# Attention with its scores in two pairs of PSUM banks, everything else in one bank, and two transposes moved from TensorE to DMA as 16-bit parts

## The chip, the core and the metric

One core of a Trainium2 chip runs the whole program. Its engines work side by side and wait for each other by semaphores: PE multiplies matrices (PEld is its weight load), DVE (vector), ACT (scalar) and POOL (GpSimd) do elementwise work, and SP only issues DMA transfers, strictly in its own order. PE writes its results to PSUM, 8 banks of 128 partitions x 512 floats; DVE and ACT can read PSUM, POOL and the DMA can't. The metric is the device time of one launch in microseconds (us).

## The reference

```python
x = x + attn(layernorm(x))        # x: 16 sequences x 512 tokens x 256, 16 heads of 16, rotary, causal softmax
x = x + ffn(layernorm(x))         # one shared SwiGLU expert and 8 routed ones, top 2, hidden 512
def attn(x):
    q, k, v = split(x @ W_attn + b_attn)
    att = softmax(where(causal, (rope(q) @ rope(k).T) / 4, -inf))
    return (att @ v) @ W_proj + b_proj
```

Inputs and outputs are float32. Only the attention half and its hand-over to the second half are touched by the change.

## The kernel before

The attention runs over 16 sequences, called batches here and `b` in the code. A batch has 4 groups (`g`) of 4 heads, and a group has 5 steps (`s`), so a batch has 20 steps, written (g, s). Every engine's program is a loop over these steps, and at each step a table says which piece of side work it does there: `QK = ((0, 4), ...)` means that the first of the four query and key projections is issued at step 4 of group 0. The tables fix each engine's order by hand; semaphores do the rest.

At every step PE issues two things first. `scores` computes queries by keys for one unit (128 x 1024) into a pair of banks, `pair_s`; the unit has causal masks added by four small matmuls. DVE takes the row maxima from it (`row_max`), and since there is one pair only, `scores` of the next unit waits for that (`max_done`). `shifted` computes keys by queries again, with the maxima as an extra row, into `pair_t`, for a group issued 8 steps earlier (`LAG = 8`); ACT takes the exponential of it (`exponentials`, to `prob`), and only then may the next `shifted` start (`exp_done`). POOL zeroes what the causal mask hides (`select`), and `mix` on PE multiplies with the values, in four pieces (`MIX`) that wait for the selects.

The maxima go back as a row: `maxima` transposes them on PE into bank 6 (`ps_m`), ACT copies them to float16 (`shift_rows`), and SP writes them with two small DMAs into the operand of `shifted` (`load_shift`).

The side work of a batch: the input of the batch after next is loaded, DVE and POOL take its mean and deviation (POOL's power operation, `input_rstd`), ACT normalises it (`normalise`). For the next batch PE transposes it (`transpose_xn`, 8 matmuls of 128 columns), ACT and DVE split it into a high and a low part of type float32r (`xn_high`, `xn_low`), and PE forms queries, keys and values as three products of the parts (`products`, L1574: 24 matmuls of 512 columns, 24 of 256). POOL splits queries and keys to 16 bits (`qk_high`, `qk_low`), and SP takes them through DRAM into place (`store_qk`, `load_qk`). For the previous batch PE transposes the outputs (`transpose_o`), DVE divides (`divide`), PE transposes back (`transpose_y`), ACT copies (`y_t`), PE multiplies in float32 with `wp` (`project_out`), DVE adds the residual (`residual`), and statistics, normalisation and a store follow. These uses have three banks of their own (`ps_q`, `ps_m`, `ps_y`).

After the last batch the pipeline drains, while SP turns stored rows by DMA for the routing, and then the feed-forward half begins.

Of the kernel before, what the change touches and what calls it, by code (L numbers as in the profile page):

```python
# [43 lines left out]
def build(nc, x, w_attn, b_attn, w_proj, b_proj, ln_scale, ln_bias, gate_w, Wg, Wu, Wd, sWg, sWu, sWd, rope, out):  # L44
# [41 lines left out]
    with ExitStack() as ctx:  # L86
# [68 lines left out]
        xh = sb_a("xh", [P, 2, T], F32R)  # L155
        xl = sb_a("xl", [P, 2, T], F32R)
# [12 lines left out]
        y_t = sb_a("y_t", [P, 2, 2, P], F32)  # L169
# [3 lines left out]
        mvb = sb_a("mvb", [P, 2, 2], F32)  # L173
# [4 lines left out]
               for k in range(2)]  # L178
# [84 lines left out]
        x_loaded = [S["x_in0"], S["x_in1"]]  # L263
        x1_stored = [S["x1_out0"], S["x1_out1"]]
# [3 lines left out]
        XN_BANK, QK_BANK, V_BANK = (ps_q, ps_y), (ps_s[0], ps_s[1], ps_o, ps_q), ps_t  # L268
# [1691 lines left out]
```

## Time and profile before

| | us |
|---|---|
| median of 3 runs (1655.62 to 1658.88) | 1657.58 |
| the profiled execution | 1656.44 |
| its span, first to last instruction | 1654.7 |
| PE busy in the span | 1513.6 |
| DVE busy | 1054.2 |
| ACT busy | 828.8 |
| POOL busy | 898.4 |

The attention takes up the first 785 us or so, the rest is the feed-forward half. Busy shares are averages over both, so the attention has to be read from its own stretch of the trace. PE's matmuls are pipelined: the time that one costs the others is the distance from its start to the start of the next, not its own duration. The other engines' durations may be added up nearly as they stand.

### The profile page before, as it was taken

How to read it: one execution, taken by the hardware profiler on the slowest of the kernel's cores; microseconds unless marked ns; L12 is line 12 of the kernel's file. 1: busy time of each engine (PE TensorE's matmuls, PEld its weight loads, DVE VectorE, ACT ScalarE, POOL GpSimd, SP SyncE). 2: the span in 40 equal slices, each digit the busy share in tenths (PEclk: the TensorE clock that was granted, in tenths of full speed). 3: DMA queues.
4: the chain of work that ended last, by engine and by line, in shares of the span. 5: the costliest groups of instructions: out<-in, count | busy, mean ns of one | idle time of the engine just before them, and what ended most of it. 6: DMA issues, size and time to landing. Idle time of an engine off the chain costs nothing.

```text
span 1654.7 us, 41571 instructions
## 1 busy us (share of the span) xinstructions
PE 1513.6 (91%) x14714; PEld 1103.3 (67%) x14716; DVE 1054.2 (64%) x1852; ACT 828.8 (50%) x1252; POOL 898.4 (54%) x1121
## 2 busy tenths in 40 slices
PE   3689999999999999987698989999999999999995
PEld 2345555555555555543586778888888898888884
DVE  7567888887888888877478777753333333333332
ACT  1266767666666666656132225544444444444442
POOL 2144555554555555544123667736766666666663
PEclk9699999999999999999699999999999999999998
DMA  2323333333233333243866854446766666666563
GB/s 83 96 91 90 116 100 113 103 109 111 90 110 111 109 108 112 91 126 94 185 176 178 194 122 98 107 107 94 109 103 98 100 100 103 99 101 100 100 102 37
DMA packets 283156, 181.03 MB, mean 109 GB/s; under 512 B 160625, under 2 KB 273649, under 8 KB 282962
## 3 DMA queue, kind: packets, MB, share of 16 engines
q1 hardware_dynamic: 244370, 130.25, 30.9%
q0 software_dynamic: 30016, 35.55, 14.6%
q10 hardware_dynamic: 8576, 12.58, 2.4%
q8 instruction: 129, 2.11, 0.6%
q14 instruction: 65, 0.53, 0.1%
HBM read 83.91 MB, written 60.17 MB: 87 GB/s over the span
## 4 chain that ended last, share of the span: by engine, by line
PE 67%; DVE 10%; DMA 8%; SPq 5%; issue 3%; ACT 3%; POOL 3%; DVEq 0%; POOLq 0%; ACTq 0%
PE bank L1574 20%; PE pair_s L1848 13%; PE bank L1709 7%; PE bank L1848 6%; PE pair_t L1848 6%; PE pair_s L1636 4%; SPq L441 3%; PE bank L1744 3%; PE pair_t L1683 3%; DMA qk_d<-qkl 2%; ACT prob L882 2%; DVE early L1501 1%; POOL prob L684 1%; PE pair_s L1656 1%; ACT early L991 1%
## 5 line engine op out<-in xcount | busy, mean ns | idle before, releaser
L882 ACT ACTIVATE prob<-pair_t 128x1024 f32<-128x1024 f32 x320 | 327.4, 1023 | 233.3 <-PE pair_t L1683 228.4
L684 POOL TENSOR_SCALAR_AFFINE_SELECT prob<-prob 128x256 f32<-128x256 f32 (+1 forms) x448 | 198.4, 456 | 334.0 <-ACT prob L882 329.3
L807 POOL DMA_INDIRECT out_x<-ysb,tok_rows x135 | 217.6, 1612 | 158.6 <-ACT ysb L1018 105.2
L991 ACT CAST early<-early 128x512 f16<-128x512 f32 (+1 forms) x206 | 124.3, 603 | 333.6 <-DVE early L1501 333.6
L1507 DVE TENSOR_TENSOR early<-early 128x512 f16<-128x512 f32 (+1 forms) x206 | 139.1, 675 | 137.9 <-ACT early L991 137.3
L1501 DVE SCALAR_TENSOR_TENSOR early<-pair_s,h_s,sg 128x512 f32<-128x512 f32 (+1 forms) x103 | 75.3, 731 | 225.4 <-PE pair_s L1848 223.2
L766 POOL DMA_INDIRECT tok_d<-tok_w,dest_i x128 | 137.1, 1071 | 103.9 <-DVE dest_i L1426 52.8
L1574 PE MATMUL bank<-wbuf,early 128*128 x1620 | 188.7, 273 | 4.6 <-DVE early L1507 2.8
L1848 PE MATMUL pair_s<-xt,wbuf 128*128 128x256 f16 x1704 | 188.7, 267 | 0.0
L1709 PE MATMUL bank<-prob,v_op 128*32 128x512 f32 (+3 forms) x2048 | 179.1, 445 | 5.1 <-POOL prob L684 5.0
L1157 DVE TENSOR_REDUCE mx<-pair_s 128x2 f32<-128x1024 f32 x128 | 156.8, 1225 | 41.1 <-PE pair_s L1656 40.3
L1574 PEld LDWEIGHTS bank<-wbuf,early 128*128 128x128 f16 x1620 | 157.7, 98 | 24.4 <-issue 5.8
L1848 PEld LDWEIGHTS pair_s<-xt,wbuf 128*128 x1704 | 160.3, 98 | 17.5
L785 POOL DMA_INDIRECT xrow<-xhl_d,tok_rows x135 | 137.1, 1015 | 53.1 <-issue 36.6
L1636 PE MATMUL pair_s<-k_op,q_op 48*128 48x512 f16 (+3 forms) x1024 | 128.5, 310 | 34.1 <-DVE mx L1157 12.1
L1636 PEld LDWEIGHTS pair_s<-k_op,q_op 48*128 48x128 f16 x1024 | 34.8, 94 | 153.7 <-DVE mx L1157 70.2
L1683 PE MATMUL pair_t<-q_op,k_op 49*128 49x512 f16 (+3 forms) x1024 | 124.3, 300 | 11.7 <-DMA q_op<-m_row 9.6
L1160 DVE TENSOR_REDUCE mx<-pair_s 128x2 f32<-128x768 f32 x128 | 122.0, 953 | 19.0 <-PE pair_s L1656 17.6
L983 ACT ACTIVATE sg<-pair_s,silu_s 128x512 f32<-128x512 f32 (+1 forms) x103 | 69.1, 671 | 82.9 <-PE pair_s L1848 71.1
L1848 PE MATMUL pair_s<-xrow,wsh 128*128 128x256 f16 x720 | 87.2, 277 | 15.9 <-DVE early L1501 15.8
L1848 PE MATMUL bank<-xt,wbuf 128*128 128x256 f16 (+1 forms) x852 | 100.7, 268 | 0.0
L1848 PE MATMUL pair_t<-xt,wbuf 128*128 128x256 f16 (+1 forms) x852 | 100.2, 267 | 0.0
(273 smaller groups left out, 2742.8 us busy)
## 6 DMA issues: line engine op xcount, KB each, us to landing
q_op<-qk_d SPq DMA_DIRECT2D x192, 64.0 KB, 2.6
k_op<-qk_d SPq DMA_DIRECT2D x192, 64.0 KB, 2.7
x_in<-in_L_attn_x SPq DMA_DIRECT2D x16, 512.0 KB, 3.9
qk_d<-qkh SPq DMA_DIRECT2D x32, 256.0 KB, 2.2
qk_d<-qkl SPq DMA_DIRECT2D x32, 256.0 KB, 2.6
xres<-in_L_attn_x SPq DMA_DIRECT2D x16, 512.0 KB, 4.6
x_d<-x SPq DMA_DIRECT2D x32, 256.0 KB, 2.2
xhl_d<-xhl SPq DMA_DIRECT2D x32, 256.0 KB, 2.5
```

Source lines behind the costliest of these rows:

```text
L684: last = nc.gpsimd.affine_select(out=v, in_=v, compare_op=ALU.is_ge, fill=0.0, base=0, pattern=[[0, v.shape[1]], [1, P]], channel_multipli ...
L766: pool.indirect_dma_start(out=tok_d, out_offset=bass.IndirectOffsetOnAxis(ap=dest_i[:, t, k:k + 1], axis=0), in_=tok_w[:, t, k, :], in_off ...
L807: pool.indirect_dma_start(out=out, out_offset=bass.IndirectOffsetOnAxis(ap=tok_rows[:, block, 0:1], axis=0), in_=ysb[:, here], in_offset=N ...
L882: nc.scalar.activation(prob[:, half, u].rearrange("p a n -> p (a n)"), pair_t[:].rearrange("p a n -> p (a n)"), ACT.Exp, scale=exp_by).the ...
L991: nc.scalar.copy(hth2[:, par, 2 * hh:2 * hh + 2, 0:w], hb2[:, hh, 0:2 * w].rearrange("p (c n) -> p c n", c=2)).then_inc(S["hh_done"], 1)
L1157: last = nc.vector.tensor_reduce(dst[:, :, u, 3], pair_s[:], AX_X, ALU.max)
L1507: nc.vector.tensor_tensor(htl2[:, par, 2 * hh:2 * hh + 2, 0:w], hb2[:, hh, 0:2 * w].rearrange("p (c n) -> p c n", c=2), hth2[:, par, 2 * h ...
L1574: last = nc.tensor.matmul(out, a, m, start=(i == 0), stop=(i == n - 1))
L1636: nc.tensor.matmul(ps_s[a][:, lo:lo + P * (q + 1)], q_op[64 * a:64 * a + KR, par, pair, P * q:P * (q + 1)], k_op[64 * a:64 * a + KR, par, ...
L1683: last = nc.tensor.matmul(ps_t[a][:, lo:lo + n], k_op[rows, par, pair, P * k:P * (k + 1)], q_op[rows, par, pair, P * k:], start=start, sto ...
L1709: last = nc.tensor.matmul(ps_o[32 * h:32 * h + 32, P * k:], v_op[:, vpar, k, GH * gg + h, :], pr[:, unit, h % 2, lo:lo + n], start=(piece ...
L1848: last = nc.tensor.matmul(out[:, w * k:w * k + w], stationary, rows[:, x, 0:w], start=(i == 0), stop=(i == 3 * CC - 1))
```

## The change

1. Banks. The scores alternate between `pair_s` and a second pair, `pair_u`, so `scores` waits for the row maxima of the unit before the last. In exchange `maxima`, `project_qk`, `project_v`, `transpose_o` and `project_out` all use the one bank `ps_a`; each waits until the user before it has been read out.
2. Normalised rows. `transpose_xn`, `xn_high` and `xn_low` go. POOL splits each of the four tiles of `xn` into float16 high and low parts (`xn_split`: a cast and a subtraction), and one DMA transpose on SP (`xn_columns`) turns all of it. The weights' parts are float16 too; the values' weights are scaled as well, and `values` multiplies back.
3. Divided rows. `transpose_y` and the copy to `y_t` go. POOL splits each of four tiles (`y_split`), two DMA transposes a batch turn them (`y_columns`), and `project_out` becomes three float16 products with the split `wp` (24 matmuls of 256 columns a batch). Before the first batch, `output_scales` on DVE finds the scale of `wp`, after another `partition_all_reduce` on POOL.
4. The variances go straight to `mv_all`; the copy to `var_all` goes.
5. All tables are new. `LAG` is 9, `maxima` is at step 1 instead of 0, `mix` at steps 1, 3, 3, 4 instead of 0, 2, 2, 3, the statistics of the next input at (0, 3) and (0, 4) instead of (1, 0) and (1, 2), `input_shift` at (1, 2) instead of (2, 1).

```diff
-        LAG, MAXIMA, M_ROWS, M_SP, O_OUT = 8, 0, 1, 2, 3
-        MIX = (0, 2, 2, 3)
-        QK, QK_ROWS = ((0, 4), (1, 4), (2, 4), (3, 1)), ((1, 0), (2, 0), (3, 0), (3, 4))
+        LAG, MAXIMA, M_ROWS, M_SP, O_OUT = 9, 1, 1, 2, 4
+        MIX = (1, 3, 3, 4)
+        XN_SPLIT, XN_COLUMNS = ((2, 2), (3, 0), (3, 2), (3, 4)), (0, 0)
+        QK, QK_ROWS = ((0, 4), (1, 2), (1, 4), (3, 4)), ((0, 4), (1, 2), (1, 4), (3, 4))
...
+            def xn_split(n, t):
...
+                high = xn_hl[:, t, 0:C]
+                nc.gpsimd.tensor_copy(high, xn[:, t]).then_inc(S["xnh_done"], 1)
+                pool.wait_ge(S["xnh_done"], NT * n + t + 1)
+                nc.gpsimd.tensor_tensor(xn_hl[:, t, C:], xn[:, t], high, ALU.subtract).then_inc(S["xnl_done"], 1)
...
+            def xn_columns(n):
...
+                sp.dma_start_transpose(xn_t[:], xn_hl[:].rearrange("p t n -> p (t n)")).then_inc(S["xn_cols"], 16)
...
-                if some(UN * G + u):
-                    pe.wait_ge(S["max_done"], UN * G + u)
+                if some(UN * G + u - 1):
+                    pe.wait_ge(S["max_done"], UN * G + u - 1)
+                pair_k = pair_of[(UN * G + u) % 2]
...
+            for t in range(NT):
+                xn_split(1, t)
+
+            pool.wait_ge(S["wp_in"], 1)
+            nc.gpsimd.partition_all_reduce(wp_top[:], wp_max[:], P, RMAX).then_inc(S["wp_topped"], 1)
...
+            def output_scales():
+
+                dve.wait_ge(S["wp_topped"], 1)
...
             prologue_qkv()
+            output_scales()
...
+            def project_out(bp, j):
+
+                pe.wait_ge(y_turned[j], 16 * bp + 16)
...
+                    last = products(ps_a[:, 256 * t:256 * t + 256],
+                                    [((y_t[:, 4 * t + c, :], y_t[:, 4 * t + CC + c, :]), (wp_h[:, c, :], wp_l[:, c, :]))
+                                     for c in range(CC)])
```

PE, before, at the turn of a group: steps 4, 0 and the start of 1 (`pair_s` scores, `pair_t` shifted, L1574 a projection, L1669 maxima, L1709 mix).

```order
L1683 MATMUL pair_t<-q_op,k_op 128x512 [waits exp_done]
L1683 MATMUL pair_t<-q_op,k_op 128x512
L1574 MATMUL bank<-xh,wah 128x512 [waits xl_done]
...
L1636 MATMUL pair_s<-k_op,q_op 128x512 [waits max_done]
L1636 MATMUL pair_s<-k_op,q_op 128x512
L1656 MATMUL pair_s<-mask,pick 128x64 x4
L1683 MATMUL pair_t<-q_op,k_op 128x384 [waits exp_done]
L1683 MATMUL pair_t<-q_op,k_op 128x384
L1683 MATMUL pair_t<-q_op,k_op 128x128 x2
L1669 MATMUL bank<-ident,mx 16x128 [waits m_done,max_done]
L1709 MATMUL bank<-prob,v_op 32x512 [waits sel_done,v_done,o_done]
```

PE, after, at steps 0 and 1 of groups 0 and 1 (L1708 scores, L1769 shifted, L1755 maxima, L1795 mix).

```order
L1708 MATMUL pair_s<-k_op,q_op 128x512 [waits max_done,ops0]
L1708 MATMUL pair_s<-k_op,q_op 128x512
L1728 MATMUL pair_s<-mask,pick 128x64 x4
L1769 MATMUL pair_t<-q_op,k_op 128x512 [waits exp_done]
L1769 MATMUL pair_t<-q_op,k_op 128x512
L1708 MATMUL pair_u<-k_op,q_op 128x512 [waits max_done]
L1708 MATMUL pair_u<-k_op,q_op 128x512
L1728 MATMUL pair_u<-mask,pick 128x64 x4
L1769 MATMUL pair_t<-q_op,k_op 128x384 [waits exp_done]
L1769 MATMUL pair_t<-q_op,k_op 128x384
L1769 MATMUL pair_t<-q_op,k_op 128x128 x2
L1755 MATMUL bank<-ident,mx 16x128 [waits qkf_done,max_done]
```

Before, two `shifted` have a projection or `maxima` and a piece of `mix` between them; after, between those of steps 0 and 1 stand only the next scores.

POOL, after, from (2, 2) on in a middle batch (L752 select, L779 bias to the residual, L667 and L669 `xn_split`, L716 and L718 `y_split`).

```order
L752 AFFINE_SELECT prob<-prob 128x2x128
L779 TENSOR_TENSOR xres<-xres,bpb 128x256
L667 CAST xn_hl<-xn 128x256 [waits xn_done,xn_cols]
L669 TENSOR_TENSOR xn_hl<-xn,xn_hl 128x256 [waits xnh_done]
L752 AFFINE_SELECT prob<-prob 128x4x128 [waits exp_done]
L716 CAST y_hl<-y 128x256 [waits y_cols0,y_done]
L718 TENSOR_TENSOR y_hl<-y,y_hl 128x256 [waits yh_done]
L752 AFFINE_SELECT prob<-prob 128x2x128 [waits exp_done]
L716 CAST y_hl<-y 128x256 [waits y_done]
L718 TENSOR_TENSOR y_hl<-y,y_hl 128x256 [waits yh_done]
```

Before, these steps held only selects and one `xres`; the eight splits stand between the selects of groups 2 and 3.

POOL, after, in the prologue and batch 0 (L707 is the all-reduce, L657 `input_rstd`; a row that says only ISA comes before an operation of another kind than the last).

```order
L669 TENSOR_TENSOR xn_hl<-xn,xn_hl 128x256 [waits xnh_done]
L707 ISA
L707 ISA wp_top<-wp_max 128x1 [waits wp_in]
L726 CAST qkh<-qkf 128x512 [waits qks0,qkf_done]
L657 ISA [waits var_done]
L657 TENSOR_TENSOR rstd<-mv,neghalf 128x4
```

The kernel before has one such pair of ISA rows, at its first all-reduce and at the `input_rstd` behind it; this is the second.

## Rows read from the trace of the kernel before

**Rows 1.** Windows: length, busy of PE, PEld, DVE, ACT, POOL, then PEclk, DMA share, GB/s.

```profile
150.00:700.00 550.00, 530.54 (x5370) 289.81 (x5372) 467.08 (x884) 370.74 (x516) 298.56 (x528) 0.99 0.35 107
750.00:775.00 25.00, 18.82 (x200) 7.98 (x198) 19.13 (x38) 16.50 (x21) 10.20 (x21) 1.00 0.47 108
```

**Rows 2.** Timeline of ACT: start, duration, line; the copy after each group's last mix.

```profile
82.48 0.58 ACT L923 COPY o_t<-bank 128x512 f32<-128x512 f32 x1
...
706.86 0.58 ACT L923 COPY o_t<-bank 128x512 f32<-128x512 f32 x1
...
751.90 0.58 ACT L923 COPY o_t<-bank 128x512 f32<-128x512 f32 x1
762.61 0.58 ACT L923 COPY o_t<-bank 128x512 f32<-128x512 f32 x1
```

**Rows 3.** Timeline of PE, batch at 425 to 470 us.

```profile
425.50 1.97 PE L1744 MATMUL bank<-wp,y_t 128*128 128x256 f32 x8
...
435.34 0.38 PE L1683 MATMUL pair_t<-q_op,k_op 49*128 49x384 f16 x4
435.65 0.28 PE L1669 MATMUL bank<-ident,mx 128*16 128x128 f32 x1
435.86 1.06 PE L1709 MATMUL bank<-prob,v_op 128*32 128x512 f32 x8
436.86 0.39 PE L1636 MATMUL pair_s<-k_op,q_op 48*128 48x512 f16 x2
...
437.45 0.39 PE L1574 MATMUL bank<-wah,xh 128*128 128x256 f32 x1
...
439.07 0.39 PE L1636 MATMUL pair_s<-k_op,q_op 48*128 48x384 f16 x4
...
444.05 0.50 PE L1574 MATMUL bank<-xh,wah 128*128 128x512 f32 x1
...
445.65 0.39 PE L1636 MATMUL pair_s<-k_op,q_op 48*128 48x512 f16 x2
...
461.97 0.66 PE L1565 MATMUL bank<-ident,xn 128*128 128x128 f32 x4
```

**Rows 4.** Timeline of PE, feed-forward half: 24 float16 matmuls of 256 columns.

```profile
831.10 2.78 PE L1574 MATMUL bank<-wsh,early 128*128 128x256 f16 x24
```

**Rows 5.** Timeline, all engines: one unit from shifted to mix.

```profile
458.54 0.38 PE L1683 MATMUL pair_t<-q_op,k_op 49*128 49x384 f16 x4
...
458.96 1.02 ACT L882 ACTIVATE prob<-pair_t 128x1024 f32<-128x1024 f32 x1 [0.77 <-PE pair_t L1683]
...
460.15 0.77 POOL L684 TENSOR_SCALAR_AFFINE_SELECT prob<-prob 128x256 f32<-128x256 f32 x2 [0.61 <-ACT prob L882]
...
460.97 1.07 PE L1709 MATMUL bank<-prob,v_op 128*32 128x384 f32 x16 [0.22 <-POOL prob L684]
```

**Rows 6.** Groups by line and form, 250 to 650 us: times, busy, mean ns, idle before.

```profile
L1064 DVE TENSOR_TENSOR xl<-bank,xh 128x512 fp32r<-128x512 f32 x18 | 12.4, 687 | 4.7 <-ACT xh L845 4.7
...
L663 POOL TENSOR_TENSOR qkl<-qkf,qkh 128x512 f16<-128x512 f32 x36 | 41.8, 1160 | 0.0
L711 POOL TENSOR_TENSOR xres<-xres,bpb 128x256 f32<-128x256 f32 x36 | 26.2, 727 | 1.1 <-issue 1.1
L658 POOL CAST qkh<-qkf 128x512 f16<-128x512 f32 x36 | 21.9, 608 | 0.0
```

**Rows 7.** Transposes in the SP queue: ns min/median/max, first and last start.

```profile
L538 SPq DMA_TRANSPOSE x_in<-xhl_d x4: 2042/2196/2933, 730.6 to 806.6; - x4
...
L581 SPq DMA_TRANSPOSE xt<-xrow x135: 1189/1258/2330, 1091.6 to 1617.0; - x135
```

**Rows 8.** Timeline, prologue and batch 0.

```profile
38.24 1.05 POOL L620 TENSOR_TENSOR rstd<-mv,neghalf 128x4 f32<-128x4 f32 x1 [8.77 <-issue]
...
47.41 1.23 DVE L1157 TENSOR_REDUCE mx<-pair_s 128x2 f32<-128x1024 f32 x1 [3.79 <-PE pair_s L1656]
...
64.53 0.75 DVE L1043 BATCH_NORM_STATS2 st<-x_in 128x6 f32<-128x256 f32 x2 [3.67 <-DMA x_in<-in_L_attn_x]
```

More of the change, by code:

```diff
@@ L503, in body @@
                                 load_qk(n, npar, j, piece // 2, piece % 2)
+                        if nxt and prev and (g, s) == XN_COLUMNS:
+                            xn_columns(b + 1)
                         if prev and (g, s) == XRES:
@@ L863, in prologue @@
                     normalise(0, 0, t)
-                for c in range(2):
-                    xn_high(0, c, XN_BANK[c])
                 act.wait_ge(S["scales_done"], 2)
@@ L890, in shift_rows @@
                     act.wait_ge(S["mrow_in"], MROWS * (G - 2))
-                nc.scalar.activation(m_row[:, half], ps_m[0:NT * GH, 0:P], ACT.Copy, scale=1.0 / SHIFT_UNIT
+                nc.scalar.activation(m_row[:, half], ps_a[0:NT * GH, 0:P], ACT.Copy, scale=1.0 / SHIFT_UNIT
                                      ).then_inc(S["m_done"], 1)
@@ L1279, in body @@
                         if nxt:
-                            for c in range(2):
-                                if (g, s) == XN_LOW[c]:
-                                    xn_low(b + 1, c)
                             for j in range(2):
@@ L1554, in _, with columns @@
         def _(pe):
-            def transpose_xn(n, c, out=None):
-                pe.wait_ge(S["xn_done"], n + 1)
-                if out is None:
-                    out = ps_q
-                    if c:
-                        pe.wait_ge(S["xl_done"], 2 * n + c)
-                    else:
-                        pe.wait_ge(S["qkl_done" if n == 1 else "qkf_done"], 4 * n)
-                for t in range(NT):
-                    last = nc.tensor.transpose(out[:, P * t:P * (t + 1)], xn[:, t, P * c:P * (c + 1)], ident[:])
-                last.then_inc(S["xnT_in"], 1)
+            def columns(part, c):
+                return xn_t[:].rearrange("p (t a c) n -> p a c t n", a=2, c=CC)[:, part, c]
             def products(out, pairs):
@@ L1583, in project_qk @@
                 else:
-                    pe.wait_ge(S["qkf_done"], 4 * n + i)
+                    pe.wait_ge(S["m_done"], 3)
                 col = 256 * (i % 2) + P * (i // 2)
-                out = ps_q if out is None else out
+                out = ps_a if out is None else out
                 products(out[:], [((wah[:, c, col:col + P], wal[:, c, col:col + P]),
-                                    (xh[:, c, :], xl[:, c, :])) for c in range(2)]).then_inc(S["qk_in"], 1)
+                                    (columns(0, c), columns(1, c))) for c in range(2)]).then_inc(S["qk_in"], 1)
@@ L1603, in prologue @@
             def prologue():
-                for c in range(2):
-                    transpose_xn(0, c, XN_BANK[c])
                 pe.wait_ge(S["attn_w"], 2)
@@ L1610, in prologue @@
                     col = 256 * (i % 2) + P * (i // 2)
-                    last = nc.tensor.matmul(ps_m[:, i:i + 1], wa[0:1, 2, col:col + P], one[0:1, :],
+                    last = nc.tensor.matmul(bank[6][:, i:i + 1], wa[0:1, 2, col:col + P], one[0:1, :],
                                             start=True, stop=True)
```

371 lines of the change are left out of this document (218 added, 153 removed).

## The prediction

> **What bounds the kernel now.** I first read the page's busy shares by slice, and then two windows. From 150 to 700 us PE is busy 530.5 of 550 us, DVE 467.1, ACT 370.7, POOL 298.6, with PEclk at 0.99 [rows 1]. So the attention runs at PE's pace, at its upper clock level, and DVE has 15% to spare. Second, the timeline of ACT: the copy of `o_t` comes once a group. From 82.48 to 706.86 us lie 56 groups or 14 batches: 44.6 us each [rows 2]; in the 12.3 batches of the window that makes 43.1 us of busy PE, 37.9 of DVE, 30.1 of ACT and 24.2 of POOL a batch. Third, the last batch, which has no next one to project for: from 751.90 to 762.61 a group still takes 10.7 us [rows 2], with PE busy only 75% [rows 1]. There the step itself sets the pace, not the sum of PE's work. That is a warning: PE's work can go without the time going with it.
>
> What a step needs at least I read from one unit: `shifted` starts at 458.54, its exponential runs from 458.96 for 1.02, the select ends at 460.92, and `mix` starts at 460.97 [rows 5]. With some 0.06 from the end of the exponential to PE, two `shifted` can't start closer than 0.42 + 1.02 + 0.06 = 1.50 us, and a `mix` can't start sooner than 2.43 us after its `shifted`. Twenty steps by 1.50 are 30 us, so the chain binds only where PE or POOL is out of step with it.
>
> **PE's work, part by part.** All prices are distances between starts. A query or key projection takes 444.05 to 445.65 = 1.60, half of the values 437.45 to 439.07 = 1.62 [rows 3]. In float16, 24 matmuls of 256 columns last 2.78 with the last one's latency, (2.78 - 0.27) / 23 = 0.109 each [rows 4]. Half of the values has 12: 1.31. A projection has 6 of 512 columns, twice the columns, so again about 1.31. Four projections save 4 x 0.29 = 1.2 us a batch, the values 2 x 0.31 = 0.6. Sixteen transposes in four calls go, 0.6 each by the 0.66 of a call [rows 3], 2.4 in all; half of the output projection was 1.97 less some 0.07 of latency, 1.90 [rows 3], and becomes 12 x 0.109 = 1.31, so 1.2 for both. Sum: 1.2 + 0.6 + 2.4 + 1.2 = 5.4, and PE's busy 43.1 falls to some 37.7 us a batch. I take 37, since part of the busy time is matmuls held up by the clock or by each other.
>
> The trace agrees with one rule there: a weight load of the float16 matmuls is hidden behind 0.109 a matmul. But a rule of the Trainium skill ("VectorE: DVE Perf Modes", Rules for kernel authors, on the three transpose paths) gives 128x128 transposes to TensorE where the destination may be PSUM, and the DMA crossbar only otherwise. Both transposes here may go to PSUM, so the rule speaks against the change; by the rows it holds only if PE is not what is short, which is what the next parts ask.
>
> **DVE and ACT.** `xn_low` (2 of 0.69 [rows 6]) and a small copy go: DVE falls from 37.9 to about 36.3 us a batch. ACT loses four copies, 0.58 each if like those of `o_t` [rows 2]. Neither was the bound, so this gives nothing by itself; with 37 of PE and 36.3 of DVE the floor of a batch is near 38.
>
> **POOL.** Eight splits come in a batch. The trace shows none of 128x256 from float32 to float16. The cast is half of 0.61 for 512 columns, 0.30; the subtraction is bounded by half of 1.16 = 0.58 below and by 1.16 above, and the nearest row is the 0.73 of the float32 sum of 256 columns [rows 6]. I take 0.30 + 0.73 = 1.03, ends 0.88 and 1.76: 8.2 us a batch (7.0 to 14.1), so POOL goes from 24.2 to 32.4. It still has room, but a select that comes due behind a split waits up to 1.0 us.
>
> The Trainium skill ("GPSIMD Engine Reference") warns that elementwise work is about twice as slow there as on VectorE; the trace shows no such pair of one shape, and I use its rows alone.
>
> **The order and the single bank.** This is where I expect the loss. I walked through one batch with the prices above.
>
> At steps 0 and 1 of each group PE has, in the order after, scores and `shifted` only between one `shifted` and the next. A `shifted` is 435.34 to 435.65 = 0.31 [rows 3], and scores about the same: 0.6 of work in a cycle of 1.50: PE idles 0.9, once or twice a group. Before, a projection (1.60), or `maxima` (435.65 to 435.86 = 0.21) and a piece of `mix` (435.86 to 436.86 = 1.00), stood there [rows 3]. I count 0.9 once in groups 0 and 1 in full (1.8), and in groups 2 and 3 partly covered by a values half and a transpose.
>
> Each user of `ps_a` waits until the last has been read out. A readout starts some 0.1 after the last matmul and lasts 0.4 to 0.6. I count the values at (2, 0) behind the copy of `qkf` 0.35, `maxima` at (2, 1) behind `values` 0.4 to 0.7, `transpose_o` at (3, 0) 0.4, `maxima` at (3, 1) behind the divide 0.66. What is queued behind a waiting `maxima` on PE is a `mix`, then all later scores, and DVE waits for these.
>
> Pieces 1 and 2 of `mix`, at step 3, wait for selects that POOL finishes only behind a cast and a subtraction: about 1.0 in group 2 and 1.0 in group 3, and 0.4 to 0.5 in groups 0 and 1, where a 1.16 `qk_low` stands ahead.
>
> My walk gives group 0 10.1, group 1 10.7, groups 2 and 3 12.0 each: 44.8 us a batch, of which nearly 8 are stalls. Before, 44.6 included about 0.75 of waits for late DMAs (the maxima's row, operands); the longer way now given to these, `LAG` 9, takes most of that away: I leave 0.1. So 44.9 against 44.6, +0.3, in 14 batches +4 us. The second pair of score banks takes the 10.7 of the last batch's groups to about 9.9: -3.
>
> **SP and its transposes.** The queue gets anew, per batch, one transpose of 512 KB and two of 256 KB. The only 512 KB transposes in the trace lie in DRAM and take 2.2 us; those of 128 KB out of SBUF take 1.26 [rows 7]. If time went with size from the second, a 512 KB one would take 5.0 and a 256 KB one 2.5; if with the first, 2.2 and 1.2. I take the first, 4.6 us more of SP a batch. What is queued behind is `store_qk`, `load_qk` and the maxima's row, which have some 0.5 to 2.5 us of slack: hidden, unless the upper end holds.
>
> A sentence of the Trainium skill ("Advanced Engine Details and Errata", X-Bar Transpose) has such transposes as fast as ordinary DMAs; in this trace 512 KB in 2.2 us is 240 GB/s for the DRAM source, and 128 KB in 1.26 is 104 GB/s for the SBUF source, so the rule would fit the value I take and the second row leans to rival C.
>
> **The head.** In the prologue POOL does one all-reduce, and the power operation behind it runs at 38.24 after 8.77 us idle that the profile lays to "issue" [rows 8]; its input had been there for 7.5 of these. The order shows the same pair of ISA rows a second time: an all-reduce, then `input_rstd` of batch 2. DVE's `output_scales` stands before the first row maxima, which ran at 47.41 [rows 8], so they wait for the second all-reduce: between 0.5 (its work alone) and 7.5 (like the power operation). Then the power operation of batch 2 can come 7.5 late, with `input_shift` now at (1, 2), soon behind it. The statistics are moved up to (0, 3), and already before they waited 3.67 for the load at 64.53 [rows 8]; the load will be issued some 2.2 later, behind `xn_columns(1)`, a transpose of 512 KB [rows 7]. Sum: about 3 + 2 + 4 = +9, ends 0 and +16. The drain: the tail works at SP's pace and at that of a chain of small steps: 0, ends -4 and +3.
>
> **Sum.** 1656.4 (the profiled execution, 1.2 below the median of 1657.58) + 4 - 3 + 9 + 0 = 1666.4; **1666 us**.
>
> **Rivals.** A: the forecast, chance 0.50, own range 1650 to 1685 (ends of the head, and 44.3 to 45.5 a batch).
> B: the stalls hide. The second pair lets DVE and PE run a step apart, so a late `mix` costs nothing while scores go on. For it: DVE's 36.3 and PE's 37 leave 7 us a batch, and a PE busy at 96% is what has held the rest back. Against it: PE's order is fixed, so a `mix` that waits stops the scores behind it. It would give 41 a batch, halfway between the floor of 38 and my 44.8: (44.6 - 41) x 14 = -50; with +9 and -3 some 1613. Chance 0.30.
> C: on the slow side, one mechanism: the transposes out of SBUF cost 5.0 and 2.5 on SP. They then make 10 us more of SP a batch, not 4.6, and the maxima's row behind `y_columns` comes after its slack of 0.5 to 2.5, stopping `shifted` for 2 us a batch or more. This decides once a 256 KB transpose takes more than about 2.5. 1666 + 14 x 2 = 1694. Chance 0.12.
> D: gains and losses cancel: 44.3 a batch with a head of +7, 1657. Chance 0.08.
>
> **How the numbers follow.** Within 0.2%, 3.3 us, is about what a measurement can't tell from no change. Faster: B's 0.30 and 0.02 of A's lower end, 0.32. Same: D and 0.02 of A, 0.10. Slower: 0.46 of A and C's 0.12, 0.58. The range that leaves out 2 in 10 reaches into B below and C above: 1615 to 1700.
>
> **What would show it.** In the changed trace: `o_t` copies 11.2 us apart in the middle; PE busy about 83% there, with idle before L1795 laid to selects and before L1755 to readouts; L1769 waiting for the exponentials at steps 0 and 1; splits of about 0.3 and 0.73; `y_t` transposes of 1.2 and 2.2 on SP; the first row maxima at 50 or later, and batch 2's power operation late. It is wrong if groups come under 10.7 apart (B), if `shifted` waits for `m_row` (C), or if a select needn't wait for splits at all.

## The result, and the profile after

The median of four runs is 1684.75 us (1682.07 to 1688.16); that of the kernel before, on the same chip, 1656.69. The ratio is 1.0178, with a 95% interval of 1.0159 to 1.0197: slower by 28 us, where +9.6 was forecast. Between the two profiled executions the span grows from 1654.7 to 1680.3, by 25.6.

The windows of the kernel after, with the columns of [rows 1]:

```profile
150.00:700.00 550.00, 472.25 (x5212) 221.11 (x5211) 451.81 (x828) 345.92 (x463) 387.38 (x719) 1.00 0.47 129
784.80:808.00 23.20, 15.93 (x133) 6.46 (x127) 16.43 (x48) 14.09 (x17) 9.56 (x19) 0.76 0.41 103
808.00:844.30 36.30, 19.69 (x398) 17.19 (x395) 11.92 (x29) 4.64 (x6) 7.77 (x12) 0.50 0.93 189
```

Against the first row of [rows 1], PE has gone from 530.54 us of busy time to 472.25, and POOL from 298.56 to 387.38. A batch takes 45.16 us (below), so PE is busy 38.8 us in each (forecast 37), DVE 37.1 (36.3), POOL 31.8 (32.4). PE really lost 4 us of work a batch, and no engine is full. The other two rows are the drain: from the last row maxima to the last `o_t` copy, and from there to the first matmul of the feed-forward half. PE is granted 0.76 in the first and 0.50, its lower level of 1.2 GHz, all through the second. The same two stretches of the kernel before had 1.00 and 0.65:

```profile
763.70:783.50 19.80, 14.33 (x126) 6.75 (x124) 13.85 (x43) 11.50 (x14) 7.35 (x17) 1.00 0.42 107
783.50:818.60 35.10, 20.38 (x399) 18.22 (x400) 16.52 (x40) 7.49 (x10) 5.93 (x6) 0.65 0.90 181
```

The view of groups by line, over the whole program, has the following for PE; all three groups exist only in the attention. The columns after the bar are busy time, mean ns, idle time before them and what ended it:

```profile
L1795 PE MATMUL bank<-prob,v_op 128*32 128x512 f32 (+3 forms) x2048 | 180.8, 448 | 42.9 <-POOL prob L752 39.9
L1769 PE MATMUL pair_t<-q_op,k_op 49*128 49x512 f16 (+3 forms) x1024 | 124.1, 300 | 41.9 <-ACT prob L947 32.4 <-DMA q_op<-m_row 6.2
L1755 PE MATMUL bank<-ident,mx 128*16 128x128 f32 x64 | 17.7, 277 | 15.9 <-DVE y L1244 9.2 <-DVE v_op L1129 6.7
```

`mix` waits 42.9 us, nearly all for selects; `shifted` 41.9, most of it for exponentials; `maxima` 15.9, for the divide and the values to leave the single bank. In the kernel before the same three groups, in the same view, waited 5.1, 11.7 and 1.7:

```profile
L1709 PE MATMUL bank<-prob,v_op 128*32 128x512 f32 (+3 forms) x2048 | 179.1, 445 | 5.1 <-POOL prob L684 5.0
L1683 PE MATMUL pair_t<-q_op,k_op 49*128 49x512 f16 (+3 forms) x1024 | 124.3, 300 | 11.7 <-DMA q_op<-m_row 9.6 <-ACT prob L882 1.8
L1669 PE MATMUL bank<-ident,mx 128*16 128x128 f32 x64 | 17.8, 279 | 1.7 <-DVE x L1186 0.9
```

So the work that PE lost came back as waits. The timeline of ACT in the kernel after, where [rows 2] were read before:

```profile
592.04 0.58 ACT L988 COPY o_t<-bank 128x512 f32<-128x512 f32 x1
...
604.46 0.58 ACT L988 COPY o_t<-bank 128x512 f32<-128x512 f32 x1
...
614.68 0.58 ACT L988 COPY o_t<-bank 128x512 f32<-128x512 f32 x1
...
624.79 0.58 ACT L988 COPY o_t<-bank 128x512 f32<-128x512 f32 x1
...
637.05 0.58 ACT L988 COPY o_t<-bank 128x512 f32<-128x512 f32 x1
```

The groups take 12.4, 10.2, 10.1 and 12.3 us, 45.0 in all: the sizes of the forecast (two of 12.0, one of 10.1, one of 10.7).

Where the 25.6 us lie I read from the row maxima of each group's last unit (DVE L1230 after, L1163 before), which mark the same work in both traces. Groups 8 and 56, before and then after:

```profile
149.91 1.23 DVE L1163 TENSOR_REDUCE mx<-pair_s 128x4 f32<-128x1024 f32 x1
...
684.99 1.23 DVE L1163 TENSOR_REDUCE mx<-pair_s 128x4 f32<-128x1024 f32 x1
```

```profile
161.56 1.21 DVE L1230 TENSOR_REDUCE mx<-pair_s 128x4 f32<-128x1024 f32 x1
...
703.51 1.23 DVE L1230 TENSOR_REDUCE mx<-pair_s 128x4 f32<-128x1024 f32 x1 [0.54 <-PE pair_s L1728]
```

| from the start of the trace | before | after | more | forecast |
|---|---|---|---|---|
| to group 8 (head) | 149.91 | 161.56 | +11.7 | +9 |
| 12 batches, to group 56 | 535.1 | 541.95 | +6.9 | +4 (14 batches, with the next row) |
| the rest of batch 14, to group 59 | 34.0 | 36.1 | +2.2 | |
| the last batch, to group 63 | 44.7 | 45.1 | +0.4 | -3 |
| to the first feed-forward matmul (drain) | 55.0 | 59.6 | +4.6 | 0 |
| the rest | 836.1 | 835.9 | -0.2 | 0 |

The loop is 44.59 us a batch before and 45.16 after.

**The head.** Timeline of the kernel after, prologue and batch 0:

```profile
29.13 0.38 POOL L677 PARTITION_ALL_REDUCE qk_top<-qk_max  x1 [5.60 <-issue]
...
44.61 1.05 POOL L657 TENSOR_TENSOR rstd<-mv,neghalf 128x4 f32<-128x4 f32 x1 [7.47 <-issue]
...
57.62 0.38 POOL L707 PARTITION_ALL_REDUCE wp_top<-wp_max  x1 [6.06 <-issue]
...
59.26 1.62 SPq L439 DMA_TRANSPOSE xn_t<-xn_hl  x1
...
60.28 1.22 DVE L1224 TENSOR_REDUCE mx<-pair_s 128x2 f32<-128x1024 f32 x1
...
64.11 0.43 SPq L429 DMA_DIRECT2D x_in<-in_L_attn_x  x1
71.64 0.75 DVE L1098 BATCH_NORM_STATS2 st<-x_in 128x6 f32<-128x256 f32 x2 [6.61 <-DMA x_in<-in_L_attn_x]
...
82.86 1.05 POOL L657 TENSOR_TENSOR rstd<-mv,neghalf 128x4 f32<-128x4 f32 x1 [14.50 <-issue]
```

The first row maxima come 12.9 us later than in [rows 8]. The first all-reduce stood at 21.80 before, now at 29.13, after 5.60 of issue: the splits of the first batch stand ahead of it. The second one comes at 57.62 with another 6.06. The load of batch 2's input goes out at 64.11 behind the transpose of 59.26, and the statistics on DVE wait 6.61 for it. The power operation of batch 2, on POOL, runs at 82.86, 7.1 us after DVE had its input ready (75.79), again under "issue". At the row maxima that end group 0 the kernel after is 16.2 us late (72.31 against 56.12), and by group 8 it has made up 4.5 of them.

**A step in the loop.** Timeline of the kernel after, one unit of group 2, the counterpart of [rows 5]:

```profile
507.55 0.38 PE L1769 MATMUL pair_t<-q_op,k_op 49*128 49x384 f16 x4
...
507.97 1.02 ACT L947 ACTIVATE prob<-pair_t 128x1024 f32<-128x1024 f32 x1 [0.49 <-PE pair_t L1769]
508.36 0.40 POOL L716 CAST y_hl<-y 128x256 f16<-128x256 f32 x1
...
508.84 0.67 POOL L718 TENSOR_TENSOR y_hl<-y,y_hl 128x256 f16<-128x256 f32 x1
...
509.46 0.77 POOL L752 TENSOR_SCALAR_AFFINE_SELECT prob<-prob 128x256 f32<-128x256 f32 x2
...
510.28 1.07 PE L1795 MATMUL bank<-prob,v_op 128*32 128x384 f32 x16 [0.84 <-POOL prob L752]
```

From `shifted` to `mix` it takes 2.73 us, not the 2.43 of [rows 5]: the split ends 0.5 after the exponential, and PE waits 0.84 in all. A split costs 1.07 us on POOL (0.40 and 0.67), forecast 1.03.

**SP.** Its queue in the kernel after, 150 to 700 us (ns min/median/max, first and last start):

```profile
L439 SPq DMA_TRANSPOSE xn_t<-xn_hl x13: 1674/2029/2992, 154.5 to 696.5; - x13
L515 SPq DMA_TRANSPOSE y_t<-y_hl x25: 1240/1242/1397, 151.3 to 693.2; - x25
```

2.03 us for 512 KB and 1.24 for 256 KB: the value taken from the first row of [rows 7] (2.2 and 1.2), not the 5.0 and 2.5 of rival C.

**The last batch.** Timeline of the kernel after:

```profile
752.83 3.14 SPq L575 DMA_TRANSPOSE x_in<-xhl_d  x1
753.12 0.27 ACT L956 ACTIVATE m_row<-bank 16x128 f16<-16x128 f32 x1 [0.69 <-PE bank L1755]
...
759.07 1.37 SPq L471 DMA_DIRECT2D q_op<-m_row  x2
...
762.18 0.39 PE L1769 MATMUL pair_t<-q_op,k_op 49*128 49x512 f16 x2 [3.75 <-DMA q_op<-m_row]
```

The row of maxima was ready at 753.4 (753.12 + 0.27). SP was in the routing's transpose until 756, other loads followed, and the row went out at 759.07. Groups 60 to 63 take 9.97, 8.86, 15.66 and 10.64 us, in the kernel before 9.73, 13.18, 10.91 and 10.92. With one pair in the order after (e3 below) they take 10.25, 11.40, 14.20 and 11.30: the second pair is worth 2.0 us here, and the wait of 3.75 gives it back. The same row is late once already in batch 14, where `shifted` waits 1.48 us for it at 715.01; the rest of the 2.2 us there I did not trace. The kernel before had the wait of the last batch too, shorter, and it stands in the group of 13.18:

```profile
739.48 0.57 PE L1683 MATMUL pair_t<-q_op,k_op 49*128 49x512 f16 x2 [2.49 <-DMA q_op<-m_row]
```

### The profile page after: what moved, and what is told of

Its sections match the earlier page's. It is cut to its first block, busy times and chain, and to the rows that moved or that the text cites. A ratio compares the mean times of both kernels' runs of the same rounds, so it can differ in the third digit from the quotient of the medians.

```text
span 1680.3 us, 41589 instructions
## 1 busy us (share of the span) xinstructions
PE 1448.4 (86%) x14586; PEld 1016.6 (61%) x14588; DVE 1042.5 (62%) x1798; ACT 800.7 (48%) x1189; POOL 1022.4 (61%) x1378
## 4 chain that ended last, share of the span: by engine, by line
PE 53%; POOL 11%; DVE 10%; DMA 8%; ACT 8%; issue 7%; SPq 3%; POOLq 0%; DVEq 0%; ACTq 0%
PE bank L1633 14%; PE pair_s L1927 13%; PE bank L1927 6%; PE pair_t L1927 6%; PE pair_u L1633 6%; POOL prob L752 5%; ACT prob L947 4%; PE bank L1795 4%; SPq L463 2%; DMA qk_d<-qkl 2%; DMA xres<-in_L_attn_x 2%; POOL qkl L731 2%; DVE early L1569 1%; ACT qkf L917 1%; DVE v_op L1129 1%
## 5 line engine op out<-in xcount | busy, mean ns | idle before, releaser
L752 POOL TENSOR_SCALAR_AFFINE_SELECT prob<-prob 128x256 f32<-128x256 f32 (+1 forms) x448 | 194.2, 447 | 226.4 <-ACT prob L947 226.1
L1795 PE MATMUL bank<-prob,v_op 128*32 128x512 f32 (+3 forms) x2048 | 180.8, 448 | 42.9 <-POOL prob L752 39.9
L1769 PE MATMUL pair_t<-q_op,k_op 49*128 49x512 f16 (+3 forms) x1024 | 124.1, 300 | 41.9 <-ACT prob L947 32.4
L1795 PEld LDWEIGHTS bank<-prob,v_op 128*32 128x32 f32 x2048 | 48.2, 109 | 114.8 <-POOL prob L752 71.8
L1633 PE MATMUL bank<-wbuf,early 128*128 x852 | 105.0, 273 | 4.6 <-DVE early L1575 3.9
L1927 PE MATMUL pair_s<-xrow,wsh 128*128 128x256 f16 x720 | 87.1, 276 | 15.9 <-DVE early L1569 15.2
L1569 DVE SCALAR_TENSOR_TENSOR early<-bank,h_s,sg 128x512 f32<-128x512 f32 (+1 forms) x103 | 75.4, 733 | 32.6 <-PE bank L1927 32.1
L1633 PE MATMUL pair_u<-wbuf,early 128*128 x768 | 94.3, 273 | 0.0
L1224 DVE TENSOR_REDUCE mx<-pair_s 128x2 f32<-128x1024 f32 x64 | 78.1, 1220 | 23.7 <-PE pair_s L1728 23.7
L1633 PEld LDWEIGHTS bank<-wbuf,early 128*128 128x128 f16 x852 | 82.3, 98 | 16.1 <-issue 6.1
```

Of the source, the lines that this page charges most:

```text
L752: last = nc.gpsimd.affine_select(out=v, in_=v, compare_op=ALU.is_ge, fill=0.0, base=0, pattern=[[0, v.shape[1]], [1, P]], channel_multipli ...
L1569: nc.vector.scalar_tensor_tensor(out=hb2[:, hh, 0:2 * w], in0=ps_up[hh][:, 0:2 * w], scalar=h_s[:, r:r + 1], in1=sg[:, hh, 0:2 * w], op0=A ...
L1633: last = nc.tensor.matmul(out, a, m, start=(i == 0), stop=(i == n - 1))
L1769: last = nc.tensor.matmul(ps_t[a][:, lo:lo + n], k_op[rows, par, pair, P * k:P * (k + 1)], q_op[rows, par, pair, P * k:], start=start, sto ...
L1795: last = nc.tensor.matmul(ps_o[32 * h:32 * h + 32, P * k:], v_op[:, vpar, k, GH * gg + h, :], pr[:, unit, h % 2, lo:lo + n], start=(piece ...
L1927: last = nc.tensor.matmul(out[:, w * k:w * k + w], stationary, rows[:, x, 0:w], start=(i == 0), stop=(i == 3 * CC - 1))
```

## The experiments

All ratios are to the kernel before, run beside them on the same chip; its medians there were 1653.01 (first four), 1655.09 (next four), 1655.03 (e9, e10) and 1653.62 (e11, e12), so differences to the kernel after, whose own neighbour had 1656.69, are good to 3 or 4 us. Each experiment has one trace. "Batch" is the mean of the 12 batches as above; after has 45.16.

**e1: one all-reduce.**

```diff
+dve.wait_ge(const_in, 48); tensor_reduce(qk_max[:, 3:4], wp, ...)   # ahead of the first all-reduce
-pool.partition_all_reduce(wp_top, wp_max)
+wp_top = qk_top[:, 3:4]
```

> The maximum of wp becomes a fourth column of the first all-reduce; the second all-reduce on POOL goes, output_scales stays where it is. Theory head: the second all-reduce (57.62 us, after 6.06 idle laid to issue) is what the first row maxima at 60.28 wait for, behind output_scales on DVE. Then the first row maxima come at about 53 us (loads of the operands land at 52), and the whole is 7 us faster than the changed kernel, 1.678 ms in place of 1.685. Rival: the loads, the later statistics or the pipeline's first batches take the gain back, and the time stays within 2 us.

1685.06 us, 1.0194 (1.0169 to 1.0220), where 7 us less was expected. The first row maxima came at 54.59, 5.7 sooner, and group 0 gained nothing by it: it ended at 74.88 against 72.31. What it waits for is the load of batch 2's input, which was issued at 67.72 here and at 64.11 in the kernel after. One thing was gained: the power operation of batch 2 had no issue time and ran at 78.55, 4.3 sooner, and group 8 came at 159.65, 1.9 sooner. The batch was longer, 45.64, and took that back.

**e2: e1, with the all-reduce ahead of the splits.**

```diff
-for t in range(NT): xn_split(0, t)
 pool.partition_all_reduce(qk_top, qk_max)
+for t in range(NT): xn_split(0, t)
```

> As e1, and the first all-reduce stands before the four splits of batch 0 on POOL, so that its 5.6 us of issue begin at 16 us, beside DVE's work on the weights, and not at 23.5. Theory head: the all-reduce runs at about 23.5 in place of 29.1, the first projection at 32 in place of 35.7 (now the splits and their transpose end last), the first row maxima near 50, and the time is 3 to 4 us below e1. Rival: the projection waits for the splits, now 4 us later, and nothing is left of it, 0.

1691.42 us, 1.0233 (1.0208 to 1.0257): 6.4 us above e1, where 3 to 4 below was expected. Timeline of POOL in this kernel:

```profile
23.23 0.39 POOL L673 PARTITION_ALL_REDUCE qk_top<-qk_max  x1 [7.32 <-DVE qk_max L1158]
23.51 0.46 POOL L666 CAST xn_hl<-xn 128x256 f16<-128x256 f32 x1
...
30.99 0.66 POOL L668 TENSOR_TENSOR xn_hl<-xn,xn_hl 128x256 f16<-128x256 f32 x1 [7.02 <-issue]
```

The all-reduce came 5.9 sooner and without issue time. The cast behind it ran at once, the subtraction waited 7.02 us. The loss is not in the all-reduce but between it and a two-operand operation, either way round; here it went before the first projection. Group 8 came at 162.38, 2.7 later than in e1; where the rest of the 6.4 went was not looked for.

**e3: one pair of score banks in the order after.**

```diff
-pe.wait_ge(max_done, UN * G + u - 1); pair_k = pair_of[(UN * G + u) % 2]
+pe.wait_ge(max_done, UN * G + u);     pair_k = pair_s
```

> The changed kernel with all scores in pair_s again, so that scores wait for the row maxima of the unit just before; all else is as in the changed kernel. Theory A (the selects, the exponentials and the single bank hold PE up, not the row maxima): a batch gets 0.3 to 0.8 us longer than 45.2, the whole 5 to 12 us slower. Theory that the second pair carries the kernel: 2 us a batch or more, 30 us slower.

1693.59 us, 1.0240 (1.0215 to 1.0265); batch 45.56. The second pair is worth some 9 us in this order (8.8 by the medians, 10 by the ratios). PE at 150 to 700 us:

```profile
L1708 PE MATMUL pair_s<-k_op,q_op 48*128 48x384 f16 (+3 forms) x776 | 94.7, 302 | 46.8 <-DVE mx L1224 32.3 <-DVE mx L1228 14.5
```

Scores wait 46.8 us, but the 24.5 of `shifted` in this window fall to 0.7, and the 33.4 of `mix` to 24.4: most of the wait only stands at another line.

**e4: four idle matmuls put in front of the scores of two steps a batch.**

```diff
+if g < 2 and u == 1:
+    for _ in range(4): matmul(pair_k[:, 0], ident_h, wah[:, 0, 0:512])
```

> The changed kernel with four more float16 matmuls of 512 columns (0.87 us, about 1.0 with what surrounds them) ahead of the scores at step 1 of groups 0 and 1, where PE waits 0.84 us for the exponential. Their results are overwritten. Theory A: that time is free, PE's 2 us more a batch cost 0.1 to 0.4, the whole 2 to 6 us. Theory that PE's work bounds the kernel: +2.0 us a batch, +30 us.

1685.43 us, 1.0188 (1.0163 to 1.0212); batch 45.22. The window shows what was put in:

```profile
150.00:700.00 550.00, 493.11 (x5304) 226.69 (x5303) 452.05 (x826) 344.87 (x461) 387.81 (x720) 1.00 0.47 128
```

PE is busy 20.9 us longer than after in the same stretch, and the kernel 0.7 us slower, which the measurement can't tell from nothing: PE's idle at steps 0 and 1 is free room, as it must be if the chain sets the pace there.

**e5: subtractions of the splits on 8 of 256 columns** (the low parts of the other columns are left out and stand at zero).

```diff
-tensor_tensor(y_hl[:, j, q % 2, C:], y[:, q % 2], high, subtract)
+tensor_tensor(y_hl[:, j, q % 2, C:C + 8], y[:, q % 2, 0:8], high[:, 0:8], subtract)   # and xn_split alike
```

> The changed kernel in which the subtraction of every split on POOL covers 8 of its 256 columns, so that most of the low parts of the normalised and divided rows are left zero. It takes 0.6 us less of POOL eight times a batch. Theory A1 (the selects of groups 2 and 3 are late because they stand behind splits): groups 2 and 3 fall from 12.5 and 12.4 to about 11.5, 2 us a batch, 28 us in all. Theory A2 (the mixes wait for the chain shifted, exponential, select, of 2.43 us, with too little for PE beside it; POOL's splits are some 0.3 of it): 0.6 us a batch, 8 to 10 us in all.

1672.89 us, 1.0106 (1.0082 to 1.0130); batch 44.72, and group 0 ends 2.6 sooner. So 11.9 us hang on the subtractions, near the 8 to 10 of the second theory and far from the 28 of the first. Groups 2 and 3 still take 12.7 and 12.0 (12.6 and 12.4 in the kernel after): short splits alone don't bring groups of 10.

**e6: the head's loads and transposes in another order on SP.**

```diff
 xn_columns(0)
+load_x(2, 0)
 for j in range(2):
-    xn_columns(1)        # once, ahead of the halves
+    if j == 0: xn_columns(1)    # inside
-if nxt2: load_x(...)
+if nxt2 and b > 0: load_x(...)
```

> The changed kernel with two things moved in the queue of SP's prologue: the load of the input of batch 2 goes out right behind the first transpose, 40 us sooner, and the second transpose stands between the operands' two halves, not behind both. Theory head-SP (what group 0 of batch 0 waits for is the input of batch 2 at 71.64, loaded at 64.11 behind the second transpose, in front of the row maxima on DVE): the row maxima of group 0 end 6 to 8 us sooner than 72.31, and the time falls by 5 to 7 us. Rival (POOL's second all-reduce and its issue time set the head): nothing.

1676.85 us, 1.0128 (1.0108 to 1.0148): 7.9 us less than after. Timeline:

```profile
25.39 0.56 SPq L429 DMA_DIRECT2D x_in<-in_L_attn_x  x1
...
64.61 0.74 DVE L1100 BATCH_NORM_STATS2 st<-x_in 128x6 f32<-128x256 f32 x2
```

The statistics have no wait and start 7.0 sooner; group 8 comes at 155.12 (161.56 after), the batch is 45.05.

**e7: e6, and the maxima over partitions taken by PE and DVE** (transpose, row maximum, a product with ones) in place of both all-reduces.

> As e6, and with no all-reduce on POOL at all: the maxima of the weights and of wp go through PE (a transpose, a reduction, a product with ones), and output_scales stands behind the row maxima of unit 1. Theory head: with all-reduces gone, POOL's 5.6, 7.5 and 6.1 us of issue go; the first scale is there at 25.5 in place of 29.5, the first row maxima come at about 47 in place of 60, group 0 ends at about 60, and the time is 12 to 14 us below the changed kernel's. Rival: 5 to 7, as e6, if only SP's queue matters.

1676.73 us, 1.0122 (1.0095 to 1.0149): 8 us below the kernel after, where 12 to 14 were expected. The head does gain, as expected: the first row maxima at 49.99, group 8 at 147.42, 14.1 sooner than after and 2.5 sooner than before the change. The power operation on POOL has no issue time any more:

```profile
33.55 1.02 POOL L659 TENSOR_TENSOR rstd<-mv,neghalf 128x4 f32<-128x4 f32 x1 [2.18 <-DVE mv L1106]
```

But the batch rose to 45.95 and the total is that of e6. PE, 150 to 700 us:

```profile
L1780 PE MATMUL pair_t<-q_op,k_op 49*128 49x512 f16 (+3 forms) x768 | 92.0, 297 | 32.4 <-ACT prob L945 20.2 <-DMA q_op<-m_row 9.8
```

`shifted` waits 9.8 us for the maxima's row, 1.0 after. SP's program in the loop is the same in both. What shifts it against the steps was not settled.

**e8: `LAG` 8, `maxima` at step 0, `mix` at steps 0, 2, 2, 3, as before.**

```diff
-LAG, MAXIMA, M_SP, O_OUT, MIX = 9, 1, 2, 4, (1, 3, 3, 4)
+LAG, MAXIMA, M_SP, O_OUT, MIX = 8, 0, 1, 3, (0, 2, 2, 3)
```

> The changed kernel with LAG 8, maxima at step 0, the mixes at steps 0, 2, 2, 3 and the copy of o_t at step 3, as before the change; all other tables stay. The waits for the shared bank are named anew for this order. Theory drain (the longer way costs a step and more at the end): from the last row maxima to the last copy of o_t 20 to 21 us in place of 23.2, but over 1 us more a batch, since the maxima's row and the bank come late: 46 to 46.5 a batch, 10 to 20 us slower in all. Rival: the drain is not shorter, since its steps are paced by other work.

1719.66 us, 1.0380 (1.0360 to 1.0401), 35 us above the kernel after, where 10 to 20 were expected; batch 48.27, not 46 to 46.5. From the last row maxima to the last `o_t` copy it took 21.63 against 23.18 after and 19.76 before. So less than half of the drain's growth hangs on these numbers, as far as one trace tells (PE was granted 0.83 in this stretch, 0.76 after and 1.00 before). The rest of the new table does not go with the shorter way.

**e9: the same program in another order.** The projections go to steps 0 and 2, one to a step, and `transpose_o` to where the bank is free, and `maxima` stands behind the `mix` of its step:

```diff
-QK, V_PROJ = ((0, 4), (1, 2), (1, 4), (3, 4)), ((2, 0), (2, 4))
+QK, V_PROJ = ((0, 2), (1, 2), (2, 0), (2, 2)), ((3, 0), (3, 2))
-XN_SPLIT, Y_SPLIT = ((2, 2), (3, 0), (3, 2), (3, 4)), ((2, 3), (2, 4), (3, 1), (3, 3))
+XN_SPLIT, Y_SPLIT = ((1, 4), (2, 2), (3, 0), (3, 3)), ((2, 3), (2, 4), (3, 3), (0, 0))
-O_T, PROJ = ((2, 2), (2, 3), (3, 0), (3, 2)), ((3, 3), (0, 2))
+O_T, PROJ = ((2, 3), (2, 4), (3, 3), (3, 4)), ((0, 0), (1, 0))
...
```

> The changed kernel (two pairs, the shared bank, splits and DMA transposes as they are, its prologue too) with other tables. Each of the eight pieces of 1.31 to 1.42 us on PE (four projections, two halves of the values, two of the output) stands at a step 0 or 2 of its own, where PE waited for the exponential or the select; the transposes of o_t stand at steps 3 and 4 of groups 2 and 3; maxima stand behind the mix of step 1, and ACT copies them at step 2, behind its exponential. Theory A (the loss lies in the order: 8 us of a batch are waits that other work could fill): a batch falls from 45.2 to 40 to 41.5, the idle time ahead of the mixes and of shifted to under half of 42.9 and 41.9 us, the whole by 50 to 70 us, to 1.62 to 1.635 ms. Rival (DVE at 37 and POOL at 32 of 45, the bank's readouts and SP's queue bound it whatever the order): 43 a batch or more, under 30 us.

1643.55 us, 0.9919 (0.9899 to 0.9939): 41 us under after, and below the kernel before. 50 to 70 us had been expected. The batch is 43.41 (expected 40 to 41.5). `mix` waits 10.2 us at 150 to 700 us, `shifted` 0.5; the scores now wait 14.8 for row maxima, and the longest wait stands at a new place, the projections:

```profile
L1652 PE MATMUL bank<-xn_t,wah 128*128 128x512 f16 x204 | 64.8, 401 | 22.8 <-DMA xn_t<-xn_hl 19.1 <-ACT m_row L975 3.7
```

**e10: e9 with the head of e7.**

> As e9, with the prologue of e7: no all-reduce on POOL, the load of batch 2 early. Theory: the head's gain of e7, 8 us in all there, adds to it: 6 to 14 us below e9. Rival: the waits for the maxima's row that took back half of it in e7 (batch 45.95 in place of 45.16) take it here too, and nothing is left.

1633.00 us, 0.9867 (0.9847 to 0.9887): the 10.6 us of the head now stay, batch 43.34.

**e11: e10 with the transpose of the normalised rows issued four steps sooner,** and its splits and normalisation before it:

```diff
-XN_COLUMNS, XN_SPLIT, NORMALISE = (0, 0), ((1, 4), (2, 2), (3, 0), (3, 3)), ((1, 3), (1, 4), (3, 0), (3, 2))
+XN_COLUMNS, XN_SPLIT, NORMALISE = (3, 4), ((1, 3), (2, 2), (3, 0), (3, 2)), ((1, 3), (1, 4), (2, 3), (3, 0))
...
```

> As e10, with the input's way shortened: normalisation and splits of the next input end a step or two sooner, its transpose on SP stands at (3, 4), behind the last half of the values, not at (0, 0), and one of y's transposes behind it. In e10 the first projection of a batch waits 18.2 us in the 550 for that transpose. Theory: those waits go, 1 to 1.5 us a batch, a batch at 42 to 42.5 in place of 43.34, the whole at 1.610 to 1.622 ms. Rival: another transfer in SP's queue (the maxima's row, the operands) comes late in its place, 1.63 ms.

1618.40 us, 0.9787 (0.9752 to 0.9822); batch 41.94. Its window and PE's groups, 150 to 700 us:

```profile
150.00:700.00 550.00, 499.71 (x5578) 235.03 (x5574) 484.32 (x870) 374.56 (x491) 409.86 (x757) 0.99 0.54 139
```

```profile
L1659 PE MATMUL bank<-xn_t,wah 128*128 128x512 f16 x200 | 60.0, 382 | 3.8 <-ACT m_row L975 3.0 <-DMA xn_t<-xn_hl 0.8
L1798 PE MATMUL bank<-prob,v_op 128*32 128x256 f32 (+3 forms) x1672 | 146.7, 445 | 20.1 <-POOL prob L771 18.9
L1772 PE MATMUL pair_t<-q_op,k_op 49*128 49x512 f16 (+3 forms) x838 | 100.9, 297 | 10.2 <-DMA q_op<-m_row 7.2 <-ACT prob L966 2.9
```

The projections' wait for the transpose is gone (19.1 in e9, 0.8 here). Some of it comes back, at `mix` (20.1) and at `shifted` (10.2), and the batch is 1.4 shorter.

**e12: e11 with one pair of score banks** (the edit of e3).

> As e11, with all scores in pair_s, as in e3. There the second pair was worth 8.8 us, since PE stood still for other reasons anyway. Theory A: with the order filled, the scores' wait for the row maxima is no longer hidden: 2 to 4 us a batch, 30 to 60 us in all, so that without the second pair the kernel is slower than the one before the change. Rival: as in e3, 0.4 a batch and under 15 us.

1719.21 us, 1.0414 (1.0368 to 1.0460), its four runs from 1710 to 1728; batch 48.07. That is 100.8 us above e11, where 30 to 60 were expected. PE, 150 to 700 us:

```profile
L1730 PE MATMUL pair_s<-k_op,q_op 48*128 48x384 f16 (+2 forms) x734 | 93.4, 311 | 81.8 <-DVE mx L1252 37.9 <-DVE mx L1250 34.5 <-DVE mx L1246 8.3
```

The scores wait 81.8 us. PE's other lines waited 43 us together in e11 and wait 4 here, so about half of what the scores wait more is hidden in waits that were there anyway; in e3 it was four fifths. PE's idle time grows from 3.8 to 7.5 us a batch. That is 3.7 of the 6.1 us by which the batch is longer; the other 2.4 are PE's work itself, 38.1 us busy a batch in e11 and 40.6 here. The granted clock is 0.95 in this window, 0.99 in e11. It falls for short stretches; in this one PE was busy for 2.38 of 5 us at 1.00, and in the next 4 us, busy all the time, it was granted 0.57, near its lower level:

```profile
304.00:309.00 5.00, 2.38 (x36) 0.94 (x33) 4.14 (x10) 2.81 (x4) 4.24 (x7) 1.00 0.51 155
309.00:313.00 4.00, 4.00 (x24) 1.19 (x20) 2.23 (x5) 2.27 (x4) 1.75 (x3) 0.57 0.71 235
```

The second pair is worth 9 us in the order of the change and 101 in this one, some two fifths of them through PE's slower work.

## Why the forecast was right in kind and short in size

**Right: the mechanism of the loop.** Less work on PE, given back as waits: the chain `shifted`, exponential, select where PE has nothing else (30.9 us of `mix` idle and 21.0 of `shifted` idle for exponentials at 150 to 700 us), and the readouts of the single bank (13.2 at `maxima`). Rounded to a batch (12.18 in the window) this is 5.3 of PE's 6.4 us of idle time, where "nearly 8" stood, and PE's work, 38.8, was put 1.8 too low. Partly by luck, then, 44.8 came near the measured 45.16: the two errors cancel. e4 and e5 bear the mechanism out: more PE work costs nothing, shorter POOL work does bring time. But selects behind splits were priced too high, at about 1.0 in group 2 and 1.0 in group 3: in e5 each subtraction takes 0.20 us in place of 0.67, by which these two delays would shrink by some 0.9 us a batch, and the batch gains 0.44. The prices of a split, of both SP transposes and of a batch on each engine held within some 10%.

**Refuted rivals.** C by the two rows of the SP queue. D by the median. B, that the stalls hide, is false for this kernel; but e9, which changes the order alone, shows that it was mostly the order that kept them in the open, not the single bank or the chain. With the same operations in each batch e11 reaches 41.94 us, near B's 41. What decided was the walk through the fixed order, not the floor of 38 that the engines' sums gave.

**The failed step** is the pricing of the ends: -3 for the last batch, 0 for the drain, +9 for the head, 6 in all. They came to +0.4, +4.6 and +11.7, 16.7 in all. Of the 15.6 us by which the traces miss the sum, 10.7 lie there and 5.1 in the loop. In parts:

- "The second pair of score banks takes the 10.7 of the last batch's groups to about 9.9": by e3 the pair does bring 2.0 us of these 3, but the row of maxima lay 5.7 us behind SP's routing transpose and loads, and PE waited 3.75. Before, that wait was there too, 2.49 us, in a group of 13.18 that I had not read when I took 10.7 for all four. I had priced the engines of the last batch and not the queue.
- The drain at 0, a term put at nothing without a price: I had counted the tail as the work of SP. It begins with the last row maxima, and from there to the last `o_t` copy it is 23.2 us against 19.8; the stretch behind adds 1.2. `LAG`, the last `mix` and the output copy all moved one step later, and e8, which takes them back, gives back 1.55 of these 3.4. PE is also granted less in both stretches (0.76 for 1.00, and 0.50 for 0.65). How much of the rest is the clock was not measured.
- The head at +9 was near, by partly wrong reasons. I laid the delay to the second all-reduce ahead of the row maxima; e1 took it away and gained nothing at group 0 and 1.9 us by group 8. The first all-reduce was late by 7.3, which I had missed: the splits ahead of it are of the kind that costs 5.6 us. And the load of batch 2's input behind `xn_columns(1)` held up the statistics, as forecast; e6 takes 7.9 us off the total. The power operation of batch 2 did come 7.1 us late, as forecast (7.5).

**The loop,** +6.9 over 12 batches, was 0.57 a batch where +0.3 had been worked out, and batch 14 added 2.2 more: 9.1 in all for the 4 of the forecast. That is the second mis-sized term, and no run splits it further. e3 adds that the second pair hid little here because `shifted` was waiting at the same time.

**Open:** what each part of the change is worth alone (no run moves only the transposes, or keeps the old tables with the new banks); why `shifted` waits more for the maxima's row in e1 and e7 (batch 45.6 and 45.95) though only the prologue differs (7.3 and 9.8 us at 150 to 700 us, 1.0 after); how much of the drain is the clock; and why the batch of e8 is 2 us longer than a walk gives.

## What to carry to other kernels

Taking work from the busiest engine gave time here only once what stays was ordered so that something runnable stands between two links of the dependent chain; count, per step, what the engine has to do while it waits, and put the side work there. A resource such as a second pair of banks has no price of its own: it was worth 9 us in one order and 101 in the other, where PE, waiting more, was also granted less clock (0.95 for 0.99). The ends of a pipeline must be priced by their queues: which DMA is issued ahead of the one that the first or last batch needs.

## What the runs showed of the hardware

POOL loses time between an all-reduce and a two-operand elementwise operation, in both directions: 5.60, 7.47, 6.06 us in the kernel after, 7.1 more behind the input of batch 2's power operation, and 7.02 in e2, marked as issue, while the cast in e2 ran at once. With no all-reduce (e7), or none since the last power operation (e1, batch 2), the power operation shows none. The Trainium skill ("GPSIMD Engine Reference", Terminology) tells of loadable kernel libraries that are brought in at run time; that would fit, and no run here shows that this is what happens.

DMA transposes out of SBUF took 2.03 us of SP's queue for 512 KB and 1.24 for 256 KB. The rule of the Trainium skill that the prediction cites ("VectorE: DVE Perf Modes", Rules for kernel authors) gives such transposes to TensorE. The change as it stood went against it and was 1.8% slower; e11 goes against it too and is 2.1% faster than the kernel with TensorE's transposes. Both have a second pair of score banks and other tables as well, so no run shows what the transposes alone are worth.
